# A banded-attention kernel: the turn of the row maxima moved from TensorE to VectorE, and their rows sent by one queue

## The chip, the cores and the metric

One core of a Trainium2 chip. The metric is the device time of one execution in microseconds (us). All times of the kernel before come from one profiled execution or from three timed runs.

## The reference, cut to what matters

```python
# x: [4, 2048, 512] float32; 16 heads of E = 32; windows of W = 128 positions, nw = 16 of them
qkv = layernorm(x) @ w_qkv
q, k, v = split(qkv)                                   # -> [B, H, nw, W, E]
k_ctx = concat([kp[:, :, i:i + nw] for i in range(3)]) # a window, the one before and the one behind
scores = einsum('bhnqe,bhnke->bhnqk', q * scale, k_ctx)
attn = softmax(where(valid, scores, -1e9), axis=-1)    # valid: inside the sequence
x = x + layernorm(einsum('bhnqk,bhnke->bhnqe', attn, v_ctx))
# then a feed-forward part: a gate g per batch from relu(x @ gate_w1.T + b) @ gate_w2.T + b,
# W1, W2 and biases mixed with 8 experts by g, out = gelu(x @ mW1.T + mb1) @ mW2.T + mb2,
x = x + layernorm(ffn(layernorm(x)))
```

The change touches the softmax alone: for each query it needs the largest score of its row before the exponential.

## The kernel before, in words

The program has three stages, one behind the other: the layernorm and the product with w_qkv (up to about 570 us), the attention (573 to 1295 us), and the gate with the mixed feed-forward part. Each of the five engine programs is written out by hand; they meet in semaphores only.

The attention runs over 16 rounds (4 batches by 4 groups of 4 heads) of 8 steps, 128 steps in all, counted by T. A step has two windows of 128 queries and 4 heads, so 8 units. Three pieces of work stand in a step, for different steps of the pipeline:

- **Scores** of the group g = T + 3 (`score`, 8 products): queries by keys, into one of three PSUM banks `ps_score`. VectorE takes the negated maximum of each query from the bank (`reduce`, the line L487), and the product three units on needs that bank again: TensorE waits for `reduced`.
- **Keys** products of the group T (`keys`): the same scores again, but turned, with keys on the partitions and queries along the free axis, so that the exponentials (`weights`, on ScalarE, L415) come out in the layout that the next product wants. The maximum of each query is subtracted by the product itself: below the 96 rows of `q_st` lies row 96 (`STACK`) with the negated maxima, against a row of ones in `k_st`. Queries reach one window past the own one, so the second half of a step's keys products needs the rows of the group T + 1.
- **Values** and **sums** of the group T - 2 (`values`, `sums`, 56 small products of 32 columns), which ScalarE copies out (`copy_out`), TensorE turns (`turn_out`) and VectorE divides by the sums (`normalise`, L499 and L503).

The maxima of the group T + 2 go from the layout "query on the partition" to a row along the free axis in each step in this way: TensorE turns the 128x8 block `neg_max` into `ps_turn[0:8, 0]` behind the values and sums (`turn_max`, L649), VectorE copies it to `max_rows` between its third and its fourth maximum (`copy_rows`, L495), and two DMAs carry it to row 96 of `q_st`, one for each window (`send_row`, L195): the first by ScalarE's queue behind its fifth exponential, the second by the sync engine's queue behind that engine's loads. The first keys products of a group wait for the second row (`rows_landed[1]`), the fifth keys product of the step before (x == 4) waits for the first row alone (`rows_landed[0]`).

The sync engine (SP) issues in a step, in this order: in even steps three loads of `k_st` and in odd steps three of `q_st` (256 KB each) and one of `v_sb` (256 KB), for the next round; the second row; and the store of the normalised output of T - 2, which waits for `norm_done`. The POOL engine adds the exponentials of neighbouring windows for the sums (`first_two`, `third`). In the last 26 steps a part of the gate stage is laid beside the attention (`along`).

Of the kernel before, what the change touches and what calls it, by code (L numbers as in the profile page):

```python
# [43 lines left out]
def attention_programs(nc, ident, eps, power, unused, x, w_qkv, qk_dram, v_dram, o_dram):  # L44
# [18 lines left out]
    with ExitStack() as ctx:  # L63
# [9 lines left out]
        neg_max = sb("neg_max", [P, 2, 2, QH], F32)  # L73
        inv_sum = sb("inv_sum", [P, 2, 2, QH], F32)
        ones = sb("ones", [P, 2, E], F32)
        max_rows = sb("max_rows", [2 * QH, 2, WIN], F32R)
# [72 lines left out]
        max_turned = sem("max_turned")  # L149
        rows_done = sem("rows_done")  # L150
        rows_landed = [[sem(f"rows_landed{i}{p}") for p in range(2)] for i in range(2)]
# [40 lines left out]
        def send_row(eng, g, i):  # L192
            w = 2 * (g % HALF) + i
            eng.wait_ge(rows_done, g + 1)
            eng.dma_start(q_st[STACK:STACK + 1, :, w * WIN:(w + 1) * WIN].bitcast(F32),  # L195
                          max_rows[QH * i:QH * (i + 1), g % 2, :].bitcast(F32)).then_inc(rows_landed[i][g % 2], 16)

        def sync(sp, along):
# [53 lines left out]
            for g in range(QKG):  # L252
                store_qk(PAIRS - 1, 1, g)
                if g == 5:
                    for i in range(2):
                        send_row(sp, 0, i)
            for i in range(2):
                send_row(sp, 1, i)
            store_v(PAIRS - 1, 1)
            for T in range(STEPS + LAG):  # L260
# [17 lines left out]
                if there(T + AHEAD - 1):  # L278
                    send_row(sp, T + AHEAD - 1, 1)
# [10 lines left out]
        def gpsimd(pool, along):  # L290
# [13 lines left out]
            for i in range(2):  # L304
                pool.memset(ones[:, i, i:i + 1], 1.0).then_inc(const_done, 1)
                pool.wait_ge(const_done, 2 + i)
            pool.wait_ge(xn_done, 1)
            pool.memset(k_st[STACK:STACK + 1, :, :].bitcast(F32), 1.0).then_inc(const_done, 1)
# [37 lines left out]
        def scalar(act, along):  # L346
# [78 lines left out]
            for T in range(STEPS + LAG):  # L425
# [5 lines left out]
                for x in range(3, UNITS):  # L431
                    if there(T):
                        weights(T, x)
                    if x == 4 and there(T + AHEAD - 1):
                        send_row(act, T + AHEAD - 1, 0)
                along(T)

        def vector(dve, along):
# [41 lines left out]
            def reduce(g, s):  # L480
# [3 lines left out]
                if s == 0 and g >= 2:  # L484
                    dve.wait_ge(max_turned, g - 1)
# [4 lines left out]
            def copy_rows(g):  # L490
                if g >= 2:
                    for i in range(2):
                        dve.wait_ge(rows_landed[i][g % 2], 16 * (g // 2))
                dve.wait_ge(max_turned, g + 1)
                dve.tensor_copy(max_rows[:, g % 2, :], ps_turn[0:2 * QH, 0, :]).then_inc(rows_done, 1)  # L495
# [38 lines left out]
            chunk(PAIRS - 1, 0)  # L534
            for g in range(GROUPS):
# [4 lines left out]
                if g == 5:  # L540
                    copy_rows(0)
                if g == 9:
                    copy_rows(1)
            for T in range(STEPS + LAG):
                if there(T + AHEAD):
                    for s in range(3):
                        reduce(T + AHEAD, s)
                if there(T + AHEAD - 1):
                    copy_rows(T + AHEAD - 1)
                if there(T + AHEAD):  # L550
                    for s in range(3, UNITS):
# [5 lines left out]
        def tensor(pe, along):  # L557
# [67 lines left out]
            def keys(g, x):  # L625
# [4 lines left out]
                if x == 0 and g % HALF == 0:  # L630
                    pe.wait_ge(rows_landed[0][g % 2], 16 * (g // 2 + 1))
                if x == 0:
                    pe.wait_ge(rows_landed[1][g % 2], 16 * (g // 2 + 1))
                if x == QH and g % HALF != HALF - 1:
                    pe.wait_ge(rows_landed[0][(g + 1) % 2], 16 * ((g + 1) // 2 + 1))
# [3 lines left out]
                else:  # L639
                    pe.wait_ge(v_done, TILES * CHUNKS + x + 1)  # L640
                pe.matmul(ps_keys[x % TRIO][:, 0:(hi - lo) * WIN], k_st[0:STACK + 1, h, w * WIN:(w + 1) * WIN],  # L641
                          q_st[0:STACK + 1, h, lo * WIN:hi * WIN], start=True, stop=True).then_inc(keys_done, 1)

            def turn_max(g):
                pe.wait_ge(reduced, UNITS * (g + 1))
                turned = g - AHEAD - LAG + 1
                if turned > 0:
# [1361 lines left out]
```

## Time and profile before

| | |
|---|---|
| median of 3 runs | 2935.1 us (2927.1 to 2939.1) |
| the profiled execution | 2943.8 us, of which the trace spans 2942.0 us |
| attention, first to last turn of the maxima | 553 to 1266 us, 128 steps |
| one step in the middle (between two copies of the maxima) | 5.2 us |
| TensorE busy | 2870.2 us, 98% of the span |
| VectorE, ScalarE, POOL busy | 1996.6, 1727.7, 854.1 us |

The trace gives each instruction's start and duration, and for each idle time of an engine what ended it. TensorE has two rows there, PE for the products and PEld for the loading of the stationary operand, which runs beside the product before it. SPq and ACTq rows are DMA issues on the queues of the sync engine and of ScalarE: their duration is that of the issue, the landing comes later.

### The profile page before, as it was taken

The numbers are of one execution on the slowest core, as the hardware profiler recorded it, in microseconds if no ns is written. First come the engines' busy times: TensorE is split into PE (matmuls) and PEld (weight loads), VectorE is DVE, ScalarE is ACT, GpSimd is POOL, SyncE is SP. The second block draws the span as 40 slices with busy tenths as digits, with TensorE's granted clock in tenths as the row PEclk, the third lists the DMA queues.
The fourth block names the chain that finished last, engine by engine and source line by source line (L and its number), as shares of the span: only waits on it lengthen the run. The fifth ranks groups of instructions, "written<-read, shape, count | busy, mean of one in ns | idle before, by whom it ended". The sixth has DMA issues, their size and how long they took to land.

```text
span 2942.0 us, 55438 instructions
## 1 busy us (share of the span) xinstructions
PE 2870.2 (98%) x20252; PEld 2380.8 (81%) x20252; DVE 1996.6 (68%) x3769; ACT 1727.7 (59%) x3385; POOL 854.1 (29%) x713
## 2 busy tenths in 40 slices
PE   8999999999999999989989999999999999999998
PEld 6888888888888887767867888788888888888886
DVE  5333333488888887878868766876768766786664
ACT  3222222377776765665636666866667666686666
POOL 1000000188888887974400000500005000040003
PEclk9999999999999999999989999999999999999999
DMA  6555555688888889959998866986769756896632
GB/s 215 184 173 171 185 186 193 218 199 201 198 194 191 201 202 214 225 176 398 390 394 325 284 209 208 356 314 203 248 211 400 270 203 200 288 399 200 232 136 86
DMA packets 361429, 697.10 MB, mean 237 GB/s; under 512 B 26576, under 2 KB 127056, under 8 KB 361184
## 3 DMA queue, kind: packets, MB, share of 16 engines
q1 hardware_dynamic: 335456, 629.63, 67.1%
q10 hardware_dynamic: 17424, 32.24, 3.1%
q0 software_dynamic: 8304, 31.98, 2.7%
q8 instruction: 150, 2.46, 0.4%
q14 instruction: 95, 0.78, 0.1%
HBM read 525.45 MB, written 167.78 MB: 236 GB/s over the span
## 4 chain that ended last, share of the span: by engine, by line
PE 84%; DVE 5%; DMA 5%; ACT 2%; issue 2%; POOL 1%; ACTq 0%; SPq 0%; DVEq 0%; POOLq 0%
PE a_acc L571 17%; PE e_hid L1390 7%; PE e_hid L1392 7%; PE e_hid L1391 7%; PE e_acc L1407 7%; PE e_acc L1409 7%; PE e_acc L1408 7%; PE a_ps_score L622 6%; PE a_ps_keys L641 6%; PE a_ps_out L670 5%; DMA a_gate_att<-o_scratch 2%; DMA a_q_st<-a_max_rows 2%; PE a_ps_out L678 2%; PE a_ps_turn L688 1%; DVE a_gate_stats L1658 1%
## 5 line engine op out<-in xcount | busy, mean ns | idle before, releaser
L1779 DVE SCALAR_TENSOR_TENSOR e_part<-e_ring,e_g_cols,e_part 128x512 f32<-128x512 f32 x896 | 648.5, 779 | 5.7 <-DMA e_ring<-mix_rows 3.3
L487 DVE TENSOR_REDUCE a_neg_max<-a_ps_score 128x1 f32<-128x384 f32 (+1 forms) x1024 | 489.6, 526 | 50.0 <-PE a_ps_score L622 48.7
L323 POOL TENSOR_TENSOR a_total<-a_probs 128x512 f32<-128x512 f32 x256 | 323.7, 1281 | 594.6 <-ACT a_probs L415 594.6
L415 ACT ACTIVATE a_probs<-a_ps_keys 128x384 f32<-128x384 f32 (+1 forms) x1024 | 423.4, 477 | 49.1 <-PE a_ps_keys L641 25.3
L1803 DVE TENSOR_TENSOR e_u_lo<-e_u,e_u_hi 128x512 fp32r<-128x512 f32 x256 | 178.7, 698 | 376.3 <-ACT e_u_hi L1538 376.2
L1534 ACT ACTIVATE e_u<-e_hid,e_mb 128x512 f32<-128x512 f32 x256 | 176.9, 691 | 434.7 <-PE e_hid L1392 422.2
L1263 POOL TENSOR_SCALAR e_var<-e_moments 128x4 f32<-128x4 f32 x15 | 6.7, 446 | 1276.9 <-DVE e_moments L1815 1276.2
L622 PE MATMUL a_ps_score<-a_k_st,a_q_st 96*128 96x384 f32 (+1 forms) x1024 | 335.5, 361 | 4.1 <-DVE a_neg_max L487 3.1
L641 PE MATMUL a_ps_keys<-a_q_st,a_k_st 97*128 97x384 f32 (+1 forms) x1024 | 318.1, 352 | 12.2 <-DMA a_q_st<-a_max_rows 11.1
L333 POOL TENSOR_TENSOR a_total<-a_total,a_probs 128x512 f32<-128x512 f32 x224 | 286.3, 1280 | 55.4 <-ACT a_probs L415 52.8
L467 DVE TENSOR_TENSOR a_qk<-a_acc,a_qk 128x512 fp32r<-128x512 f32 x128 | 88.1, 690 | 308.1 <-ACT a_qk L364 308.1
L1551 ACT ACTIVATE e_sums<-e_acc 128x512 f32<-128x512 f32 x508 | 289.1, 595 | 9.0 <-PE e_acc L1409 5.7
L1562 ACT ACTIVATE e_acc<-e_sums 128x512 f32<-128x512 f32 x448 | 263.7, 613 | 0.0
L364 ACT ACTIVATE a_qk<-a_acc 128x512 fp32r<-128x512 f32 x128 | 76.2, 598 | 258.8 <-PE a_acc L571 255.8
L622 PEld LDWEIGHTS a_ps_score<-a_k_st,a_q_st 96*128 96x128 f32 x1024 | 194.8, 191 | 40.5 <-DVE a_neg_max L487 29.0
L641 PEld LDWEIGHTS a_ps_keys<-a_q_st,a_k_st 97*128 97x128 f32 x1024 | 192.3, 192 | 28.5 <-DMA a_q_st<-a_max_rows 14.0
L571 PE MATMUL a_acc<-a_xt_hi,a_w_hi 128*128 128x512 f32 x508 | 202.5, 399 | 1.6 <-DVE a_w_lo L522 1.0
L1407 PE MATMUL e_acc<-e_wa_hi,e_u_hi 128*128 128x512 f32 x512 | 200.4, 391 | 3.3 <-DVE e_u_lo L1803 3.1
L1390 PE MATMUL e_hid<-e_y_hi,e_wb_hi 128*128 128x512 f32 x512 | 199.8, 390 | 2.5 <-DVE e_wb_lo L1798 2.5
L1407 PE MATMUL e_acc<-e_wb_hi,e_u_hi 128*128 128x512 f32 x512 | 200.1, 391 | 1.3 <-ACT e_acc L1562 1.3
L1390 PE MATMUL e_hid<-e_y_hi,e_wa_hi 128*128 128x512 f32 x512 | 200.5, 392 | 0.0
L1391 PE MATMUL e_hid<-e_y_lo,e_wa_hi 128*128 128x512 f32 x512 | 200.2, 391 | 0.0
(154 smaller groups left out, 6466.7 us busy)
## 6 DMA issues: line engine op xcount, KB each, us to landing
e_ring<-mix_rows SPq DMA_DIRECT2D x558, 512.0 KB, 5.4
qk_scratch<-a_qk SPq DMA_DIRECT2D x128, 512.0 KB, 3.2
a_k_st<-qk_scratch SPq DMA_DIRECT2D x180, 256.0 KB, 4.5
a_q_st<-qk_scratch SPq DMA_DIRECT2D x180, 256.0 KB, 4.4
v_scratch<-a_v SPq DMA_DIRECT2D x64, 256.0 KB, 3.1
a_v_sb<-v_scratch SPq DMA_DIRECT2D x64, 256.0 KB, 5.0
o_scratch<-a_out SPq DMA_DIRECT2D x128, 128.0 KB, 3.1
x_scratch<-a_gate_x POOLq DMA_DIRECT2D x16, 1024.0 KB, 10.1
```

The source lines that it names most:

```text
L323: add = pool.tensor_tensor(total[:, g % 2, i], p[0], p[1], ALU.add)
L333: pool.tensor_tensor(total[:, g % 2, i], total[:, g % 2, i], p[2], ALU.add).then_inc(summed, 1)
L415: act.activation(probs[:, m % PROBS, h, 0:(hi - lo) * WIN], ps_keys[x % TRIO][:, 0:(hi - lo) * WIN], ACT.Exp, scale=SCALE).then_inc(exp_do ...
L487: dve.tensor_reduce(neg_max[:, g % 2, i, h:h + 1], ps_score[y % TRIO][:, 0:(hi - lo) * WIN], AX_X, ALU.max, negate=True).then_inc(reduced, 1)
L571: mm = pe.matmul(out, lhs, rhs, start=(n == 0), stop=(n == len(terms) - 1))
L622: pe.matmul(ps_score[y % TRIO][:, 0:(hi - lo) * WIN], q_st[0:STACK, h, w * WIN:(w + 1) * WIN], k_st[0:STACK, h, lo * WIN:hi * WIN], start= ...
L641: pe.matmul(ps_keys[x % TRIO][:, 0:(hi - lo) * WIN], k_st[0:STACK + 1, h, w * WIN:(w + 1) * WIN], q_st[0:STACK + 1, h, lo * WIN:hi * WIN], ...
L1390: pe.matmul(hid[s % 4][:, :], w_hi(n)[:, 0, cols], y_hi[:, slot, k, :], start=(k == 0), stop=False)
L1391: pe.matmul(hid[s % 4][:, :], w_hi(n)[:, 0, cols], y_lo[:, slot, k, :], start=False, stop=False)
L1407: pe.matmul(acc[t][:, :], u_hi[:, s % 3, cols], w_hi(n)[:, 1, :], start=False, stop=False, skip_group_check=True)
L1551: act.activation(sums[:, runs[r][1], t, :], acc[t][:, :], ACT.Copy).then_inc(copied, 1)
L1779: dve.scalar_tensor_tensor(out=part[:, n % 2, half, :], in0=ring[:, slot, :], scalar=g_cols[:, b, e:e + 1], in1=so_far, op0=ALU.mult, op1= ...
```

## The change

TensorE no longer turns the maxima. VectorE does it in two instructions (`turn_max` in its program). The first multiplies the 128x8 block of maxima into a 128x4x32 tile `spread`: block b keeps the maxima of the partitions 32b to 32b + 31 alone, by a 0/1 mask of four columns that was copied once into the free columns of the PSUM bank `ps_turn`, and the rest is zero. The second turns `spread` (128x128) in blocks of 32x32, which leaves in `max_rows` four rows for each head and window, each zero outside its own 32 queries. Four rows of `q_st` (96 to 99) against four rows of ones in `k_st` then add up to what one row gave before; the keys products contract over 100 rows in place of 97.

VectorE's turn stands at the start of a step, ahead of the first of its eight maxima, and the maxima are no longer cut in two by the copy. Both rows DMAs (now of 16 pieces of 512 bytes in place of 4) are issued by SP behind its loads; ScalarE sends none. There is one semaphore for both: `rows_landed[g % 2]`, counted to 32, which the fifth keys product of the step before waits for. The set-up gains a few small memsets on POOL and one small copy on VectorE.

```diff
@@ -73,5 +73,7 @@
         neg_max = sb("neg_max", [P, 2, 2, QH], F32)
+        spread = sb("spread", [P, P // E, E], F32R)
+        own_block = sb("own_block", [P, P // E], F32)
         inv_sum = sb("inv_sum", [P, 2, 2, QH], F32)
         ones = sb("ones", [P, 2, E], F32)
-        max_rows = sb("max_rows", [2 * QH, 2, WIN], F32R)
+        max_rows = sb("max_rows", [P, 2, WIN], F32R)
         q_st = sb("q_st", [P, QH, SEQ], F32R)
@@ -148,5 +150,6 @@
         reduced = sem("reduced")
-        max_turned = sem("max_turned")
+        spread_done = sem("spread_done")
+        mask_done = sem("mask_done")
         rows_done = sem("rows_done")
-        rows_landed = [[sem(f"rows_landed{i}{p}") for p in range(2)] for i in range(2)]
+        rows_landed = [sem(f"rows_landed{p}") for p in range(2)]
         keys_done = sem("keys_done")
@@ -191,7 +194,8 @@
 
-        def send_row(eng, g, i):
-            w = 2 * (g % HALF) + i
+        def send_rows(eng, g):
             eng.wait_ge(rows_done, g + 1)
-            eng.dma_start(q_st[STACK:STACK + 1, :, w * WIN:(w + 1) * WIN].bitcast(F32),
-                          max_rows[QH * i:QH * (i + 1), g % 2, :].bitcast(F32)).then_inc(rows_landed[i][g % 2], 16)
+            for i in range(2):
+                w = 2 * (g % HALF) + i
+                eng.dma_start(q_st[STACK:STACK + P // E, :, w * WIN:(w + 1) * WIN].bitcast(F32),
+                              max_rows[i:P:E // QH, g % 2, :].bitcast(F32)).then_inc(rows_landed[g % 2], 16)
 
@@ -254,6 +258,4 @@
                 if g == 5:
-                    for i in range(2):
-                        send_row(sp, 0, i)
-            for i in range(2):
-                send_row(sp, 1, i)
+                    send_rows(sp, 0)
+            send_rows(sp, 1)
             store_v(PAIRS - 1, 1)
@@ -278,3 +280,3 @@
                 if there(T + AHEAD - 1):
-                    send_row(sp, T + AHEAD - 1, 1)
+                    send_rows(sp, T + AHEAD - 1)
                 if T == 0:
@@ -306,4 +308,12 @@
                 pool.wait_ge(const_done, 2 + i)
+            pool.wait_ge(const_done, 3)
+            pool.memset(spread[:, :, :].bitcast(F32), 0.0).then_inc(const_done, 1)
+            pool.wait_ge(const_done, 4)
+            pool.memset(own_block[:, :], 0.0).then_inc(const_done, 1)
+            for b in range(P // E):
+                pool.wait_ge(const_done, 5 + b)
+                pool.memset(own_block[b * E:(b + 1) * E, b:b + 1], 1.0).then_inc(const_done, 1)
+            pool.wait_ge(const_done, 9)
             pool.wait_ge(xn_done, 1)
-            pool.memset(k_st[STACK:STACK + 1, :, :].bitcast(F32), 1.0).then_inc(const_done, 1)
+            pool.memset(k_st[STACK:STACK + P // E, :, :].bitcast(F32), 1.0).then_inc(const_done, 1)
 
@@ -433,4 +443,2 @@
                         weights(T, x)
-                    if x == 4 and there(T + AHEAD - 1):
-                        send_row(act, T + AHEAD - 1, 0)
                 along(T)
@@ -484,3 +492,3 @@
                 if s == 0 and g >= 2:
-                    dve.wait_ge(max_turned, g - 1)
+                    dve.wait_ge(spread_done, g - 1)
                 dve.wait_ge(scored, y + 1)
@@ -489,8 +497,14 @@
 
-            def copy_rows(g):
+            def turn_max(g):
+                dve.wait_ge(reduced, UNITS * (g + 1))
+                if g >= 1:
+                    dve.wait_ge(rows_done, g)
+                dve.tensor_tensor(spread[:, :, :].rearrange("p b (h i) -> p b i h", h=QH)[:, :, 0:2],
+                                  neg_max[:, g % 2].unsqueeze(1).to_broadcast([P, P // E, 2, QH]),
+                                  ps_turn[:, 0, 0:P // E].unsqueeze(2).unsqueeze(3).to_broadcast([P, P // E, 2, QH]),
+                                  ALU.mult).then_inc(spread_done, 1)
+                dve.wait_ge(spread_done, g + 1)
                 if g >= 2:
-                    for i in range(2):
-                        dve.wait_ge(rows_landed[i][g % 2], 16 * (g // 2))
-                dve.wait_ge(max_turned, g + 1)
-                dve.tensor_copy(max_rows[:, g % 2, :], ps_turn[0:2 * QH, 0, :]).then_inc(rows_done, 1)
+                    dve.wait_ge(rows_landed[g % 2], 32 * (g // 2))
+                dve.transpose(max_rows[:, g % 2, :].bitcast(F32), spread[:, :, :].bitcast(F32).rearrange("p b c -> p (b c)")).then_inc(rows_done, 1)
 
@@ -534,2 +548,5 @@
             chunk(PAIRS - 1, 0)
+            dve.wait_ge(const_done, 10)
+            dve.tensor_copy(ps_turn[:, 0, 0:P // E], own_block[:, :]).then_inc(mask_done, 1)
+            dve.wait_ge(mask_done, 1)
             for g in range(GROUPS):
@@ -540,13 +557,10 @@
                 if g == 5:
-                    copy_rows(0)
+                    turn_max(0)
                 if g == 9:
-                    copy_rows(1)
+                    turn_max(1)
             for T in range(STEPS + LAG):
-                if there(T + AHEAD):
-                    for s in range(3):
-                        reduce(T + AHEAD, s)
                 if there(T + AHEAD - 1):
-                    copy_rows(T + AHEAD - 1)
+                    turn_max(T + AHEAD - 1)
                 if there(T + AHEAD):
-                    for s in range(3, UNITS):
+                    for s in range(UNITS):
                         reduce(T + AHEAD, s)
@@ -630,7 +644,5 @@
                 if x == 0 and g % HALF == 0:
-                    pe.wait_ge(rows_landed[0][g % 2], 16 * (g // 2 + 1))
-                if x == 0:
-                    pe.wait_ge(rows_landed[1][g % 2], 16 * (g // 2 + 1))
+                    pe.wait_ge(rows_landed[g % 2], 32 * (g // 2 + 1))
                 if x == QH and g % HALF != HALF - 1:
-                    pe.wait_ge(rows_landed[0][(g + 1) % 2], 16 * ((g + 1) // 2 + 1))
+                    pe.wait_ge(rows_landed[(g + 1) % 2], 32 * ((g + 1) // 2 + 1))
                 x += 8 * g
@@ -640,12 +652,4 @@
                     pe.wait_ge(v_done, TILES * CHUNKS + x + 1)
-                pe.matmul(ps_keys[x % TRIO][:, 0:(hi - lo) * WIN], k_st[0:STACK + 1, h, w * WIN:(w + 1) * WIN],
-                          q_st[0:STACK + 1, h, lo * WIN:hi * WIN], start=True, stop=True).then_inc(keys_done, 1)
-
-            def turn_max(g):
-                pe.wait_ge(reduced, UNITS * (g + 1))
-                turned = g - AHEAD - LAG + 1
-                if turned > 0:
-                    pe.wait_ge(norm_done, turned)
-                pe.transpose(ps_turn[0:2 * QH, 0, :], neg_max[:, g % 2].rearrange("p w h -> p (w h)"), ident[:, :])\
-                  .then_inc(max_turned, 1)
+                pe.matmul(ps_keys[x % TRIO][:, 0:(hi - lo) * WIN], k_st[0:STACK + P // E, h, w * WIN:(w + 1) * WIN],
+                          q_st[0:STACK + P // E, h, lo * WIN:hi * WIN], start=True, stop=True).then_inc(keys_done, 1)
 
@@ -683,3 +687,3 @@
                 pe.wait_ge(out_copied, g + 1)
-                pe.wait_ge(rows_done, min(g + LAG + AHEAD, STEPS))
+                pe.wait_ge(spread_done, min(g + LAG + AHEAD, STEPS))
                 if g >= 1:
@@ -723,3 +727,3 @@
             chunk(PAIRS - 1, 0)
-            pe.wait_ge(const_done, 4)
+            pe.wait_ge(const_done, 10)
             for g in range(GROUPS):
@@ -728,6 +732,2 @@
                     score(y // UNITS, y % UNITS)
-                if g == 5:
-                    turn_max(0)
-                if g == 9:
-                    turn_max(1)
             for T in range(STEPS + LAG):
@@ -742,4 +742,2 @@
                 along(T)
-                if there(T + AHEAD - 1):
-                    turn_max(T + AHEAD - 1)
                 scores(T, [3])
```

In VectorE's program, in the middle of the attention, the instructions stand before in this order (`a_neg_max` rows are the maxima, L499 and L503 the division of the output):

```order
L487 TENSOR_REDUCE a_neg_max<-a_ps_score 128x1 x3
L495 CAST a_max_rows<-a_ps_turn 8x128
L487 TENSOR_REDUCE a_neg_max<-a_ps_score 128x1 x5
L499 RECIPROCAL a_inv_sum<-a_ps_turn 128x8
L503 TENSOR_TENSOR a_out<-a_ps_turn,a_inv_sum 128x256
```

and now in this:

```order
L502 TENSOR_TENSOR a_spread<-a_neg_max,a_ps_turn 128x4x2x4
L509 STREAM_TRANSPOSE a_max_rows<-a_spread 128x128
L495 TENSOR_REDUCE a_neg_max<-a_ps_score 128x1 x8
L513 RECIPROCAL a_inv_sum<-a_ps_turn 128x8
L517 TENSOR_TENSOR a_out<-a_ps_turn,a_inv_sum 128x256
```

One copy has gone from the middle of the maxima, two instructions have come in front of them.

On the queue of the sync engine, an odd step and an even step in the middle of the attention stand before in this order:

```order
L183 DMA a_q_st<-qk_scratch 32x4x512 x3
L230 DMA a_v_sb<-v_scratch 128x4x128
L195 DMA a_q_st<-a_max_rows 1x4x128
L236 DMA o_scratch<-a_out 128x2x128
L183 DMA a_k_st<-qk_scratch 32x4x512 x3
```

and now in this:

```order
L186 DMA a_q_st<-qk_scratch 32x4x512 x3
L234 DMA a_v_sb<-v_scratch 128x4x128
L199 DMA a_q_st<-a_max_rows 4x4x128 x2
L240 DMA o_scratch<-a_out 128x2x128
L186 DMA a_k_st<-qk_scratch 32x4x512 x3
```

The row that ScalarE sent has joined the other one behind the loads, and each is four rows wide.

On ScalarE's queue one window of exponentials stands before as

```order
L415 ACTIVATE a_probs<-a_ps_keys 128x384 x2
L195 DMA a_q_st<-a_max_rows 1x4x128
L415 ACTIVATE a_probs<-a_ps_keys 128x384 x6
L422 ACTIVATE a_out_t<-a_ps_out 128x384
```

and the DMA in it is gone.

## Rows read from the trace of the kernel before

**Rows 1.** Page, part 1: engine, busy time, share of the span, instructions

```profile
PE 2870.2 (98%) x20252; PEld 2380.8 (81%) x20252; DVE 1996.6 (68%) x3769; ACT 1727.7 (59%) x3385; POOL 854.1 (29%) x713
```

**Rows 2.** Windows view, attention: PE, PEld, DVE, ACT, POOL busy; clock; DMA share

```profile
573.00:1276.00 703.00, 686.99 (x10326) 581.01 (x10326) 577.70 (x1411) 486.82 (x1152) 605.46 (x487) 0.99 0.84 200
```

**Rows 3.** Timeline of VectorE: start, us, line, tiles, count, idle before

```profile
1004.91 0.28 DVE L495 CAST a_max_rows<-a_ps_turn 8x128 fp32r<-8x128 f32 x1 [0.75 <-PE a_ps_turn L649]
...
1007.76 0.42 DVE L503 TENSOR_TENSOR a_out<-a_ps_turn,a_inv_sum 128x256 f32<-128x256 f32 x1
1008.10 1.48 DVE L487 TENSOR_REDUCE a_neg_max<-a_ps_score 128x1 f32<-128x384 f32 x3
1010.11 0.28 DVE L495 CAST a_max_rows<-a_ps_turn 8x128 fp32r<-8x128 f32 x1 [0.53 <-PE a_ps_turn L649]
1010.31 2.50 DVE L487 TENSOR_REDUCE a_neg_max<-a_ps_score 128x1 f32<-128x384 f32 x5
1012.74 0.20 DVE L499 RECIPROCAL a_inv_sum<-a_ps_turn 128x8 f32<-128x8 f32 x1
1012.97 0.42 DVE L503 TENSOR_TENSOR a_out<-a_ps_turn,a_inv_sum 128x256 f32<-128x256 f32 x1
```

**Rows 4.** Timeline of TensorE, same step: loads (PEld) and products (PE)

```profile
1009.70 0.08 PEld L649 LDWEIGHTS a_ps_turn<-ident,a_neg_max 128*8 128x8 f32 x1 [0.20 <-DVE a_neg_max L487]
1009.70 0.19 PEld L622 LDWEIGHTS a_ps_score<-a_k_st,a_q_st 96*128 96x128 f32 x1
1009.73 0.42 PE L622 MATMUL a_ps_score<-a_k_st,a_q_st 96*128 96x384 f32 x1
...
1010.90 0.19 PEld L622 LDWEIGHTS a_ps_score<-a_k_st,a_q_st 96*128 96x128 f32 x1 [0.19 <-DVE a_neg_max L487]
```

**Rows 5.** Waits view, whole span: who for whom, us, times, longest

```profile
DVE a_max_rows L495 <- PE a_ps_turn L649: 96.5, 120, 3.3
...
PEld a_ps_score L622 <- DVE a_neg_max L487: 29.0, 119, 1.9
...
PEld a_ps_keys L641 <- DMA a_q_st<-a_max_rows: 14.0, 9, 3.0
```

**Rows 6.** Timeline of SP's queue: issue start, duration

```profile
1008.21 0.38 SPq L236 DMA_DIRECT2D o_scratch<-a_out  x1
1008.64 2.67 SPq L183 DMA_DIRECT2D a_q_st<-qk_scratch  x3
1011.35 0.69 SPq L230 DMA_DIRECT2D a_v_sb<-v_scratch  x1
1012.08 0.58 SPq L195 DMA_DIRECT2D a_q_st<-a_max_rows  x1
1013.42 0.39 SPq L236 DMA_DIRECT2D o_scratch<-a_out  x1
1013.85 1.62 SPq L183 DMA_DIRECT2D a_k_st<-qk_scratch  x3
```

**Rows 7.** DMA view, windows 1000.5:1000.9 and 1011.2:1011.6: issues, us to landing

```profile
a_v_sb<-v_scratch SPq DMA_DIRECT2D x1, 256.0 KB, 4.8
...
a_v_sb<-v_scratch SPq DMA_DIRECT2D x1, 256.0 KB, 4.9
```

**Rows 8.** Timelines: v load issued on SP, keys products of the next step on PE

```profile
1000.62 0.43 SPq L230 DMA_DIRECT2D a_v_sb<-v_scratch  x1
...
1005.09 0.51 PE L641 MATMUL a_ps_keys<-a_q_st,a_k_st 97*128 97x384 f32 x2
...
1015.56 0.51 PE L641 MATMUL a_ps_keys<-a_q_st,a_k_st 97*128 97x384 f32 x2
```

**Rows 9.** Timeline of ScalarE and its queue

```profile
1010.73 0.58 ACTq L195 DMA_DIRECT2D a_q_st<-a_max_rows  x1
```

**Rows 10.** Lines by form, VectorE: L1679 and L1658 in 573:1276, then L1679 behind 1300

```profile
L1679 DVE SCALAR_TENSOR_TENSOR a_gate_shift<-a_gate_moments,a_gate_rstd 128x4 f32<-128x4 f32 x2 | 5.5, 2760 | 0.0
L1658 DVE BATCH_NORM_STATS2 a_gate_stats<-a_gate_att 128x6 f32<-128x512 f32 x12 | 8.2, 682 | 0.0
...
L1679 DVE SCALAR_TENSOR_TENSOR a_gate_shift<-a_gate_moments,a_gate_rstd 128x4 f32<-128x4 f32 x13 | 2.5, 196 | 0.4
```

More of the change, by code:

```diff
@@ L540, in vector @@
                 if g == 5:
-                    copy_rows(0)
+                    turn_max(0)
                 if g == 9:
-                    copy_rows(1)
+                    turn_max(1)
             for T in range(STEPS + LAG):
+                if there(T + AHEAD - 1):
+                    turn_max(T + AHEAD - 1)
                 if there(T + AHEAD):
-                    for s in range(3):
-                        reduce(T + AHEAD, s)
-                if there(T + AHEAD - 1):
-                    copy_rows(T + AHEAD - 1)
-                if there(T + AHEAD):
-                    for s in range(3, UNITS):
+                    for s in range(UNITS):
                         reduce(T + AHEAD, s)
@@ L742, in tensor @@
                 along(T)
-                if there(T + AHEAD - 1):
-                    turn_max(T + AHEAD - 1)
                 scores(T, [3])
```

## The prediction, on record before the changed kernel ran

> **What bounds the kernel now.** I read the page's first part, then the attention alone by its windows, then three steps of it as a timeline, engine by engine, and last the waits and the DMA landings. TensorE is busy 98% of the span [rows 1], and in the attention 687.0 of 703 us, at a granted clock of 0.99, its upper level of 2.4 GHz. VectorE has 577.7 us there, ScalarE 486.8, POOL 605.5, and the DMA engines are busy to 84% [rows 2]. So TensorE sets the end. Outside the attention the change has only small set-up work that lies beside 500 us of other stages; I cost it at nothing.
>
> The reader is to see two things in the step that begins with the copy at 1004.91 and ends with the next at 1010.11, 5.20 us on [rows 3]. First, VectorE waits: 0.53 us before the copy L495, for TensorE's turn of the maxima, which stands behind all values and sums; 96.5 us in all, 120 times [rows 3, 5]. Second, TensorE pays for it a little later. The fourth score product has run from 1009.73 to 1010.15 [rows 4], but its maximum starts at 1010.31, behind the copy [rows 3]. The seventh score product needs that bank: its load of operands waits 0.19 us, until 1010.90 [rows 4]. Such waits are 29.0 us in 119 cases, nearly one for each of the 128 steps [rows 5]. They are what the change can give back to TensorE.
>
> **TensorE's turn.** 128 products of 128x128 against an 8-column operand go. The trace says that they hid well: the loads of the turn and of the score product behind it both start at 1009.70, and the score product starts 0.03 us later [rows 4]. Without the turn that score product must first load its own operand, 0.19 us long, which now lies partly under the turn. So I take 0.0 us for the turn, with 0 and 0.1 us as bounds; a little of this may show, but not 0.28 us a step.
>
> **The copy.** Without it the fourth maximum can start when its score product has ended, 1010.15 plus about 0.04 us of signalling (my estimate: 1012.97 - 1012.74 - 0.20 = 0.03 between the two dependent instructions of rows 3), so at 1010.18 in place of 1010.31 [rows 3, 4]. The seventh score product moves by the same 0.13 us, and of its wait of 0.19 us some 0.06 stays. Bounds: 0 and 0.19 us a step. I take 0.13: over about 124 steps (128 without the first and last few) **-16 us**.
>
> **VectorE's new work** must fit. A step now holds, from start to start: five maxima 2.43 us (1010.31 to 1012.74), reciprocal 0.23, division 0.34 (1007.76 to 1008.10), three maxima about 1.40: 4.40 us [rows 3]. New are the mask product, 32 elements a partition from PSUM, and the turn, 128 elements from SBUF. For the first the nearest rows are the reciprocal, 0.20 us, and the division, 0.42 us for 256 elements [rows 3]: 0.20 plus 0.03 for the wait between the two. For the second: the copy of 128 elements, 0.28 us, of which 0.20 show up to the next start (1010.11 to 1010.31) [rows 3], and 0.68 us for the statistics over 512 elements [rows 10]. I take 0.25 us, as it is nearest to the copy. Together 0.5 us, at worst 0.9. That gives 4.9 us of a 5.07 us step, still in front of the bound; at 0.9 us VectorE would need 5.3 and the gain is gone in narrow steps (+0.1 us each). The maxima that wait behind it are the first three of the step, which TensorE needs only after its values and sums. Cost 0 at the value taken.
>
> **ScalarE** loses a DMA issue of 0.58 us [rows 9]. Its exponentials are not what TensorE waits for in these rows; I take nothing for it.
>
> **The rows on SP's queue.** Here the change costs. Before, the fifth keys product of a step waited only for the first row, issued by ScalarE at 1010.73 [rows 9]. The row that SP issues at 1012.08, behind three q loads and one v load [rows 6], was needed half a step later still. Now both stand behind the loads, and both are needed at the fifth keys product. In an odd step: the v load is issued at 1011.35 and lands 4.9 us later, at 1016.25; the keys pair with the fifth product started at 1015.56 [rows 6 to 8]. In the pair of steps before it: 1000.62 + 4.8 = 1005.42 against 1005.09 [rows 7, 8]. If the rows land no earlier than the load ahead of them they are 0.7 and 0.3 us late, 0.5 on average, and the second DMA may add up to its own issue, 0.58 us [rows 6]. If they overtake it they are in time. A row DMA is 8 KB against 256 KB, so I do not charge the whole landing, and take half: 0.25 us late against the old time, bounds 0 and 1.1 us. Even steps carry no v load and their rows can leave when the k loads are issued, which is earlier than before; I take nothing. The odd wait cannot be made up: the q loads start behind a store that waits for the end of VectorE's step two steps before (1008.21) [rows 6], so rows, fifth keys product, end of step and next odd step are one ring. Of it only the part behind the fifth keys product gets 0.13 us shorter. Per pair of steps the ring gives 0.25 - 0.13 = +0.12 us where TensorE alone would give -0.26. Over 62 pairs: **+7 us** in place of -16. VectorE's earlier turn does not help an odd row, since that waits for SP, not for `rows_done`.
>
> **The sum.** 2943.8 us of the profiled execution + 7 = 2951; that execution lies 8.7 us above the median of the three runs, 2935.1, so for the median I forecast **2942 us**. Less than 0.5% (about 15 us) cannot be told from no change here.
>
> **Rivals.**
>
> *The rows come in time.* Then only the gain stands: -16 us, 2919 us. For it: in the kernel before the rows delayed loads of keys products 9 times only (14.0 us) [rows 5]. Against: that wait was for a row that had left 0.6 us before the v load [rows 6, 9]. Chance 0.22.
>
> *The rows wait in full.* 0.5 us late, -0.13, over 62 pairs: +23 us, 2958 us; with the second DMA's 0.58 us whole: +59 us, 2994 us. This is the case that ends slower. It decides from 0.13 us of lateness on. For it speaks the DMA share of 84% [rows 2], which leaves few gaps to overtake in. Chance 0.2.
>
> *VectorE's turn waits for POOL.* In the attention POOL adds nearly without a pause (605 of 703 us) [rows 2]. An instruction of VectorE with two inputs in SBUF took 2.76 us there and 0.20 us where POOL is idle, while the statistics, with one input, took 0.68 [rows 10]. The mask product reads one of its inputs from PSUM, as the division does, whose 0.42 us are steady. The turn has one input, but source and target are both SBUF. Should it be held like L1679, by 0.6 us or more, VectorE needs 5.5 us a step: some +0.35 us over 124 steps, +43 us, 2978 us, and twice that if POOL loses as much. Since the statistics are not held, chance 0.1.
>
> The Trainium skill ("SBUF — State Buffer", SBUF: two separate sides) says that VectorE and GpSimd share a port pair as an exclusive lock for VectorE instructions in a two-port mode or with two SBUF inputs. By that rule, the trace agrees: L1679 is held, L1658 is not. The skill's "Vector Engine (DVE) Microarchitecture Reference" (5.1) lists copy, cast and tensor_scalar as enabled for that mode and not the turn, which speaks against this rival; its "VectorE: DVE Perf Modes" (The three transpose paths) gives 311 ns for a 128x128 bf16 turn, with which the sum would be the same.
>
> *The forecast*, some lateness that about eats the gain: chance 0.48.
>
> **How the numbers follow.** Faster by over 0.5% (under 2920 us) needs nearly the whole gain: most of the first rival, 0.17. Slower (over 2950): the second and third rival nearly whole and an end of the forecast's, 0.34. The rest, 0.49, is within 0.5%. The range goes from a little below the first rival, 2916, to between the second one's two prices, 2972; what lies outside is about 0.08 below and 0.12 above.
>
> **What would show it.** In the new profile: no L649; a turn and a mask product on VectorE of about 0.25 and 0.2 us; fewer than 29 us of waits of score products for maxima; VectorE's idle time in the middle of a step down from 96.5 us; and, as the test of the forecast, waits of keys products for the rows at each second step, of some 0.2 to 0.5 us, 20 us or so in all. Steps of 5.07 us with no such wait would mean that the first rival holds. A turn of 0.8 us or more would mean the third. I would be wrong altogether if TensorE's turn did cost more than it seems, or if ScalarE's freed 0.58 us brought the exponentials, and with them the keys products, forward.

## The result and the profile after

The changed kernel takes 2946.3 us (median of 8 runs, 2944.8 to 2952.4) against 2933.8 us of the kernel before in 8 runs beside it: a ratio of 1.0042, 95% interval 1.0032 to 1.0051, some 12 us slower. The forecast for the same comparison was +7 us. The profiled execution spans 2950.6 us, 8.6 more than before; below, "the trace" is that one. It is the slowest of its eight runs, 6 us above their median, and the trace of before is of a run 10 us above its median, so the medians, and not two spans, say what the change costs.

The page's first part, the answer to [rows 1]:

```profile
PE 2859.3 (97%) x20124; PEld 2382.3 (81%) x20124; DVE 2024.2 (69%) x3898; ACT 1727.7 (59%) x3385; POOL 855.9 (29%) x719
```

TensorE has 128 instructions and 11 us of busy time less, VectorE 129 instructions and 28 us more. VectorE's new pair, from the lines view of the attention (573 to 1290 us):

```profile
L509 DVE STREAM_TRANSPOSE a_max_rows<-a_spread 128x128 f32<-128x128 f32 x126 | 39.2, 311 | 4.4
L502 DVE TENSOR_TENSOR a_spread<-a_neg_max,a_ps_turn 128x32 fp32r<-128x32 f32 x126 | 25.7, 204 | 0.1
```

0.31 and 0.20 us, with a spread of no more than 0.04 us over all 128. VectorE's timeline in a step with 40 values products (most steps have 48 and are some 0.2 us longer), to be read against [rows 3], whose step also has 40:

```profile
1016.07 0.20 DVE L502 TENSOR_TENSOR a_spread<-a_neg_max,a_ps_turn 128x32 fp32r<-128x32 f32 x1
1016.30 0.31 DVE L509 STREAM_TRANSPOSE a_max_rows<-a_spread 128x128 f32<-128x128 f32 x1
1016.54 1.45 DVE L495 TENSOR_REDUCE a_neg_max<-a_ps_score 128x1 f32<-128x384 f32 x3
1018.15 2.52 DVE L495 TENSOR_REDUCE a_neg_max<-a_ps_score 128x1 f32<-128x384 f32 x5 [0.16 <-PE a_ps_score L636]
1020.58 0.20 DVE L513 RECIPROCAL a_inv_sum<-a_ps_turn 128x8 f32<-128x8 f32 x1
1020.82 0.42 DVE L517 TENSOR_TENSOR a_out<-a_ps_turn,a_inv_sum 128x256 f32<-128x256 f32 x1
1021.16 0.20 DVE L502 TENSOR_TENSOR a_spread<-a_neg_max,a_ps_turn 128x32 fp32r<-128x32 f32 x1
```

From pair to pair 5.09 us, where the step of [rows 3] took 5.20; the fourth maximum waits only for its own score product, and a step without a late row is about 0.1 us shorter. The waits of the attention, in the order of [rows 5] (who for whom, us, times, longest):

```profile
DVE a_neg_max L495 <- PE a_ps_score L636: 93.9, 167, 3.3
...
PEld a_ps_keys L653 <- DMA a_q_st<-a_max_rows: 47.0, 40, 3.6
...
PEld a_ps_score L636 <- DVE a_neg_max L495: 13.6, 63, 0.8
...
PEld a_ps_keys L653 <- ACT a_probs L425: 3.9, 14, 0.6
```

The waits for maxima have halved, 29.0 to 13.6 us. The waits for the rows have gone from 14.0 to 47.0 us. Of these, counted step by step in the timelines, 43.6 us in 38 of the 40 cases are for rows that SP sent in an odd step, and 19.5 us in 10 cases lie behind 1110 us, mostly where the gate's part runs beside the attention. In full at one place: SP's queue, then TensorE's loads of operands in the step that needs those rows.

```profile
1070.34 2.52 SPq L186 DMA_DIRECT2D a_q_st<-qk_scratch  x3
1072.91 0.43 SPq L234 DMA_DIRECT2D a_v_sb<-v_scratch  x1
1073.38 1.14 SPq L199 DMA_DIRECT2D a_q_st<-a_max_rows  x2
1075.22 0.39 SPq L240 DMA_DIRECT2D o_scratch<-a_out  x1
```

```profile
1077.21 0.19 PEld L636 LDWEIGHTS a_ps_score<-a_k_st,a_q_st 96*128 96x128 f32 x1
1078.63 0.30 PEld L653 LDWEIGHTS a_ps_keys<-a_q_st,a_k_st 100*128 100x128 f32 x2 [1.23 <-DMA a_q_st<-a_max_rows]
```

The rows had been ready in SBUF since 1070.35 (the turn started at 1070.04 and took 0.31). The DMA view of that moment gives the v load in front of them 5.2 us to landing:

```profile
a_v_sb<-v_scratch SPq DMA_DIRECT2D x1, 256.0 KB, 5.2
```

1072.91 + 5.2 = 1078.11, and the keys product goes on at 1078.63: the profile has no landing of the rows themselves, but the wait for them ends only after the load has landed, not before it. The chain of work that ended last, cut to 573 to 1276 us, before and after (its shares by line):

```profile
by line: PE a_ps_score L622 25.0%; PE a_ps_keys L641 23.5%; PE a_ps_out L670 22.9%; DMA a_q_st<-a_max_rows 7.4%; PE a_ps_out L678 7.2%; PE a_ps_turn L688 5.4%; PE a_ps_turn L649 3.2%; DVE a_neg_max L487 1.6%; issue 1.1%; ACT a_probs L415 0.
```

```profile
by line: DMA a_q_st<-a_max_rows 21.0%; PE a_ps_score L636 15.4%; PE a_ps_keys L653 15.3%; PE a_ps_out L674 12.8%; SPq L186 8.3%; issue 4.8%; DVE a_neg_max L495 4.3%; PE a_ps_out L682 4.0%; PE a_ps_turn L692 3.2%; SPq L199 2.4%; SPq L234 2.0
```

Before, TensorE's own work made up most of the chain, and the rows' DMA 7.4% of it. Now it runs for a fifth of the time through the rows' DMA, and with 8.3% through SP's issue of loads (L186), as it should if rows, keys product and loads form the ring over two steps that the prediction describes.

### The profile page after: what moved, and what is told of

Read it like the earlier page. It is cut to its first block, busy times and chain, and to the rows that moved or that the text cites. A ratio compares the mean times of both kernels' runs of the same rounds, so it can differ in the third digit from the quotient of the medians.

```text
span 2950.6 us, 55211 instructions
## 1 busy us (share of the span) xinstructions
PE 2859.3 (97%) x20124; PEld 2382.3 (81%) x20124; DVE 2024.2 (69%) x3898; ACT 1727.7 (59%) x3385; POOL 855.9 (29%) x719
## 4 chain that ended last, share of the span: by engine, by line
PE 76%; DMA 8%; DVE 6%; SPq 3%; issue 3%; ACT 2%; POOL 2%; ACTq 0%; DVEq 0%; POOLq 0%
PE a_acc L585 17%; PE e_acc L1405 7%; PE e_hid L1388 7%; PE e_hid L1389 7%; PE e_hid L1390 7%; PE e_acc L1407 7%; PE e_acc L1406 7%; DMA a_q_st<-a_max_rows 5%; PE a_ps_score L636 4%; PE a_ps_keys L653 4%; PE a_ps_out L674 3%; DMA a_gate_att<-o_scratch 3%; SPq L186 2%; DVE a_neg_max L495 1%; POOL a_gate_x L1229 1%
## 5 line engine op out<-in xcount | busy, mean ns | idle before, releaser
L653 PE MATMUL a_ps_keys<-a_q_st,a_k_st 100*128 100x384 f32 (+1 forms) x1024 | 317.6, 352 | 36.4 <-DMA a_q_st<-a_max_rows 35.1
L636 PE MATMUL a_ps_score<-a_k_st,a_q_st 96*128 96x384 f32 (+1 forms) x1024 | 325.0, 358 | 1.4 <-DVE a_neg_max L495 1.3
L653 PEld LDWEIGHTS a_ps_keys<-a_q_st,a_k_st 100*128 100x128 f32 x1024 | 190.2, 191 | 54.4 <-DMA a_q_st<-a_max_rows 47.0
L1406 PE MATMUL e_acc<-e_wa_lo,e_u_hi 128*128 128x512 f32 x512 | 200.1, 391 | 0.0
```

Of the source, the lines that this page charges most:

```text
L636: pe.matmul(ps_score[y % TRIO][:, 0:(hi - lo) * WIN], q_st[0:STACK, h, w * WIN:(w + 1) * WIN], k_st[0:STACK, h, lo * WIN:hi * WIN], start= ...
L1406: pe.matmul(acc[t][:, :], u_hi[:, s % 3, cols], w_lo(n)[:, 1, :], start=False, stop=False, skip_group_check=True)
```

## The experiments

All ratios are to the kernel before, run beside each kernel on the same chip. The waits are those of one traced execution each. Theory A: the rows on SP's queue behind its loads eat a real gain. Theory B: VectorE's turn or the four-row pieces cost the time.

**Who sends the first row** (e1). ScalarE sends it again, behind its fifth exponential:

```diff
+                    if x == 4 and there(T + AHEAD - 1):
+                        send_rows(act, T + AHEAD - 1, (0,))
-                    send_rows(sp, T + AHEAD - 1)
+                    send_rows(sp, T + AHEAD - 1, (1,))
```

with the separate semaphores and waits of before.

> The changed kernel, with the first row of each step sent by ScalarE's queue behind its fifth exponential as before, the second by the sync engine behind its loads, and the old separate waits. Theory A (the rows that must pass SP's loads eat the gain): the waits of the keys products for the rows fall from 47 us back to about 14, the steps without a wait keep their length (5.3 us in place of 5.42), so about 25 us less than the changed kernel: a ratio to the kernel before of about 0.995. Theory B (VectorE's turn itself, or the four-row pieces, cost the time): the ratio stays at 1.003 to 1.005. ScalarE has its issue of 0.58 us back; if that issue was what held the keys products, the ratio is 1.00.

Measured: 2931.5 us, ratio 0.9992 (0.9983 to 1.0001). Some 15 us back, but not the 0.995 that A expected; it is the third outcome of the expectation, 1.00. Nor is all of it the queue's doing, since this kernel has the separate waits too: with them alone the ratio is already 1.0006 (e4 below), so that the other queue is worth 0.14%, little more than the noise of the two ratios. Its waits:

```profile
PEld a_ps_keys L658 <- DMA a_q_st<-a_max_rows: 24.9, 24, 2.7
...
PEld a_ps_keys L658 <- ACT a_probs L425: 11.9, 59, 0.6
```

The waits for rows do not fall to 14 us, and the keys products now wait 11.9 us for exponentials, 59 times, where the changed kernel has 3.9. ScalarE's issue (0.55 us in that trace) is not hidden here. It wasn't wholly hidden before either: that kernel has 7.0 us of the same waits, and with ScalarE's issue taken out (e3 below) 2.8. The waits for maxima are 13.3 us here, as low as in the changed kernel, with ScalarE's issue back: that gain does not come from the missing issue.

**Rows ahead of the loads** (e2).

```diff
             for T in range(STEPS + LAG):
+                if there(T + AHEAD - 1):
+                    send_rows(sp, T + AHEAD - 1)
...
-                if there(T + AHEAD - 1):
-                    send_rows(sp, T + AHEAD - 1)
                 if T == 0:
```

> The changed kernel, with both rows issued by the sync engine ahead of its loads of the same step in place of behind them. Theory A: hardly any wait of the keys products for rows outside the last 26 steps, so the whole gain shows: 12 to 18 us less than the kernel before, a ratio of 0.994 to 0.996, and below the run with ScalarE's row if its issue costs anything. Theory B: 1.003 to 1.005. A third outcome: the loads, now 1.6 us later, become what the score products wait for; then waits for q and k loads appear and the ratio is 1.00 or more.

Measured: 2923.6 us, ratio 0.9965 (0.9952 to 0.9979), the span of its trace 2913.2 us. The traced run is the fastest of the five, 9 us below their median, so its waits are the kernel's at its best.

```profile
PEld a_ps_score L636 <- DVE a_neg_max L495: 14.1, 64, 0.9
...
PEld a_ps_score L636 <- DMA a_q_st<-qk_scratch: 7.0, 5, 2.5
...
PEld a_ps_keys L653 <- DMA a_q_st<-a_max_rows: 4.3, 4, 1.4
```

The same DMAs, the same queue, the same VectorE: only the order on the queue differs, and 43 us of waits for rows and 0.8% of the time (23 us) are gone. A had expected 0.994 to 0.996; the waits for q loads in the middle line are part of the third outcome. Theory B falls here: the turn costs 0.31 us in this trace too, and pieces of four rows are in it as well.

**One part of the change alone** (e3): the kernel before, TensorE's turn kept, both rows by SP behind its loads, two semaphores.

```diff
-                    send_row(sp, T + AHEAD - 1, 1)
+                    for i in range(2):
+                        send_row(sp, T + AHEAD - 1, i)
-                    if x == 4 and there(T + AHEAD - 1):
-                        send_row(act, T + AHEAD - 1, 0)
```

> The kernel before, with one part of the change alone: both rows are sent by the sync engine behind its loads, each with its own semaphore, and ScalarE sends none. TensorE still turns the maxima. Theory A: this alone costs; the fifth keys product now waits for a row behind the v load at part of the odd steps. Each is one row and not four, and the steps are 0.1 us longer, so less than the 33 us more of waits in the changed kernel: 10 to 25 us more than before, a ratio of 1.003 to 1.009. Theory B: within 0.2% of the kernel before.

Measured: 2938.7 us, 1.0015 (1.0006 to 1.0024): slower, clear of noise, but by less than the 1.003 that A asked for at least, and inside the 0.2% of B. Taken alone this run does not decide between them. Its waits for rows are 20.7 us in 25 cases, 14.0 in 9 before; the waits for maxima (24.3) stay near the 29.0 of before.

**Two waits in place of one** (e4), on the changed kernel.

```diff
-                    pe.wait_ge(rows_landed[g % 2], 32 * (g // 2 + 1))
+                    pe.wait_ge(rows_landed[0][g % 2], 16 * (g // 2 + 1))
+                if x == 0:
+                    pe.wait_ge(rows_landed[1][g % 2], 16 * (g // 2 + 1))
                 if x == QH and g % HALF != HALF - 1:
-                    pe.wait_ge(rows_landed[(g + 1) % 2], 32 * ((g + 1) // 2 + 1))
+                    pe.wait_ge(rows_landed[0][(g + 1) % 2], 16 * ((g + 1) // 2 + 1))
```

> The changed kernel with one semaphore for each of the two row DMAs again: the fifth keys product waits for the first DMA alone, the second one is waited for at the first keys product of its step. Both are still sent by the sync engine behind its loads. If the second DMA is what comes late (it is issued 0.57 us behind the first), a good part of the 33 us of added waits goes: a ratio near 0.998. If both land together, behind the loads, hardly anything changes: 1.002 to 1.004. I expect the second.

Measured: 2937.4 us, 1.0006 (0.9996 to 1.0017), with 31.9 us of waits for rows. I had expected 1.002 to 1.004, and it is 0.36% better than the changed kernel: the wait for the second DMA, which the fifth keys product doesn't need, makes up about 10 of the 12 us lost.

**The joint wait without the wide rows** (e7): e3 with the fifth keys product waiting for both DMAs.

```diff
-                    pe.wait_ge(rows_landed[0][(g + 1) % 2], 16 * ((g + 1) // 2 + 1))
+                    for i in range(2):
+                        pe.wait_ge(rows_landed[i][(g + 1) % 2], 16 * ((g + 1) // 2 + 1))
```

> The kernel before, with both rows sent by the sync engine behind its loads, and the fifth keys product waiting for both, as in the changed kernel; the turn is TensorE's, each DMA carries one row. Against the run in which that product waited for the first DMA alone (1.0015): if waiting for the second DMA is worth about 10 us here too, as it was with the four-row pieces, 1.004 to 1.006. If the four-row pieces are what makes the second DMA late, 1.0015 to 1.003.

Measured: 2943.9 us, 1.0030 (1.0019 to 1.0041). The joint wait costs 0.15% here and 0.36% with pieces of four rows; each is a difference of two ratios with intervals of 0.1%. That it costs is shown for the wide rows; for single rows it is at the edge of the noise, and that wide rows make it worse is not shown.

**TensorE's turn put back, its result unused** (e5), on e2.

```diff
+            def idle_turn(g):
+                pe.wait_ge(spread_done, g + 1)
...
+                pe.transpose(ps_turn[0:2 * QH, 1, :], neg_max[:, g % 2].rearrange("p w h -> p (w h)"), ident[:, :])
...
                 along(T)
+                if there(T + AHEAD - 1):
+                    idle_turn(T + AHEAD - 1)
```

> The kernel with both rows ahead of the loads (ratio 0.9965), and TensorE's turn of the maxima put back where it stood, its result unused: 126 products more, nothing waits for them. The prediction costed that turn at nothing, with 0.1 us as bound. By it: within 2 us of the kernel with the rows ahead, 0.9965 to 0.997. If the turn did cost TensorE what a 128-column product takes in a dense run (0.11 us, from the spacing of the three output turns), 12 to 14 us more: 1.001.

Measured: 2924.1 us, 0.9955 (0.9938 to 0.9972). 126 turns cost nothing that can be told: from the low end of e2's interval to the high end of this one it is 6 us, an estimate of 0.05 us a turn at most. Taking them from TensorE gained nothing by itself. The waits for maxima stay low (6.0 us) with the turn back.

**Rows ahead, with TensorE's late turn** (e8): e3 with both sends at the head of SP's step.

```diff
             for T in range(STEPS + LAG):
+                if there(T + AHEAD - 1):
+                    for i in range(2):
+                        send_row(sp, T + AHEAD - 1, i)
                 if T == 2:
```

> The kernel before, with both rows sent by the sync engine ahead of its loads, nothing else changed. TensorE's turn comes 1.4 to 1.8 us later in a step than VectorE's, so the loads behind the rows start some 1.9 us plus 1.2 us of issues later than in the kernel before. Theory A (the early turn on VectorE is what makes rows ahead of the loads worth it): waits for q, k or v loads appear or the steps keep their 5.4 us, ratio 0.999 to 1.006. Theory C (the order on the queue is all, whoever turns): 0.9965 as with VectorE's turn.

Measured: 2963.2 us, 1.0093 (1.0078 to 1.0108), worse than every other kernel and than A's 1.006. SP's queue, and the waits:

```profile
1000.81 0.44 SPq L236 DMA_DIRECT2D o_scratch<-a_out  x1
1002.90 1.21 SPq L195 DMA_DIRECT2D a_q_st<-a_max_rows  x2
1004.15 1.39 SPq L183 DMA_DIRECT2D a_q_st<-qk_scratch  x3
```

```profile
PEld a_ps_score L621 <- DMA a_q_st<-qk_scratch: 37.5, 41, 4.7
```

SP stands idle from 1001.25 to 1002.90 for the late rows, the loads behind them start that much later, and the score products wait 37.5 us for loads of q, while the waits for rows are down to 0.3 us. In e2 the same gap is 0.1 us:

```profile
1003.45 0.38 SPq L240 DMA_DIRECT2D o_scratch<-a_out  x1
1003.92 1.16 SPq L199 DMA_DIRECT2D a_q_st<-a_max_rows  x2
1005.13 1.72 SPq L186 DMA_DIRECT2D a_q_st<-qk_scratch  x3
```

So theory C (order alone) falls: it takes the early turn and the early place on the queue together. That the early turn has to be VectorE's is not shown; TensorE's turn was not tried at an earlier place.

**Rows between the q and the v loads** (e10).

```diff
+                if there(T + AHEAD - 1):
+                    send_rows(sp, T + AHEAD - 1)
                 n, c = divmod((T - 5) // 2, 4)
                 if T >= 5 and T % 2 == 1 and n + 1 < ROUNDS:
                     sp.wait_ge(pv_done, T - 2)
                     load_v(n + 1, c)
-                if there(T + AHEAD - 1):
-                    send_rows(sp, T + AHEAD - 1)
```

> The changed kernel, with both rows behind the three k or q loads as before but ahead of the v load of the odd steps. The prediction priced a late row by the landing of the v load in front of it. If that is the load that matters, most of the 47 us of waits for rows goes: a ratio of 0.997 to 0.999. If a row is late behind any load, since the DMA engines are still busy with the q loads, about half of them stay: 1.000 to 1.003.

Measured: 2931.7 us, 0.9991 (0.9980 to 1.0003), between the two outcomes, with 21.0 us of waits for rows in 22 cases. Passing the one v load gives back 0.5% of 0.8%, so it is the load that matters most. The rest is not the q loads' alone: about half of these waits, 10.3 us in 9 cases, are for rows sent in even steps, behind the k loads.

**VectorE's turn between the maxima** (e6), where the copy stood.

```diff
-                if there(T + AHEAD - 1):
-                    turn_max(T + AHEAD - 1)
                 if there(T + AHEAD):
-                    for s in range(UNITS):
+                    for s in range(3):
+                        reduce(T + AHEAD, s)
+                if there(T + AHEAD - 1):
+                    turn_max(T + AHEAD - 1)
+                if there(T + AHEAD):
+                    for s in range(3, UNITS):
                         reduce(T + AHEAD, s)
```

> The changed kernel, with VectorE's mask product and turn between the third and the fourth maximum, where the copy stood, in place of ahead of the first. VectorE idles 0.38 us there in the changed kernel and the two take 0.47 us. If the gain in steps without a late row (5.42 to 5.31 us) comes from the fourth maximum no longer standing behind a copy, half of it or more goes, since the turn now stands there: 3 to 8 us more than the changed kernel, 1.005 to 1.007. The rows of odd steps wait for the loads anyway. If the gain comes from ScalarE's missing issue or from TensorE's missing turn, the ratio stays at 1.004.

Measured: 2944.9 us, 1.0026 (1.0014 to 1.0038). I expected it slower than the changed kernel, and it is not; the waits for maxima are 13.7 us, as low as there. Its timeline says why:

```profile
1001.84 1.48 DVE L495 TENSOR_REDUCE a_neg_max<-a_ps_score 128x1 f32<-128x384 f32 x3
1003.23 0.20 DVE L502 TENSOR_TENSOR a_spread<-a_neg_max,a_ps_turn 128x32 fp32r<-128x32 f32 x1
1003.47 0.31 DVE L509 STREAM_TRANSPOSE a_max_rows<-a_spread 128x128 f32<-128x128 f32 x1
1004.13 2.54 DVE L495 TENSOR_REDUCE a_neg_max<-a_ps_score 128x1 f32<-128x384 f32 x5 [0.36 <-PE a_ps_score L639]
```

The turn starts as the third maximum ends and is over before the fourth one's score product is. What delayed the fourth maximum before was not that something stood there, but that the copy waited for TensorE's turn, which came behind the values and sums. Of the other sources of the gain, e5 rules out TensorE's turn as such, and e1 ScalarE's issue.

**Rows ahead in odd steps alone** (e12).

```diff
             for T in range(STEPS + LAG):
+                if T % 2 == 1 and there(T + AHEAD - 1):
+                    send_rows(sp, T + AHEAD - 1)
...
-                if there(T + AHEAD - 1):
+                if T % 2 == 0 and there(T + AHEAD - 1):
                     send_rows(sp, T + AHEAD - 1)
```

> The changed kernel, with the rows ahead of the loads in odd steps alone (those with q loads and the v load) and behind the k loads in even steps. With both ahead (0.9965) score products waited 7.0 us for q loads in 5 cases. If only the odd steps had late rows, this is as fast as with both ahead or up to 5 us faster: 0.995 to 0.997. If even steps had late rows too, waits for rows come back: 0.998 to 1.000.

Measured: 2926.9 us, 0.9965 (0.9953 to 0.9978), the same as e2. But the waits for rows are back:

```profile
PEld a_ps_keys L655 <- DMA a_q_st<-a_max_rows: 21.0, 19, 4.5
```

Of these 21.0 us, 20.5 in 18 cases are for rows sent in even steps, behind the k loads. One of them: its rows leave SP at 1035.25 and the keys product goes on 5.8 us later.

```profile
1033.76 1.44 SPq L186 DMA_DIRECT2D a_k_st<-qk_scratch  x3
1035.25 1.14 SPq L199 DMA_DIRECT2D a_q_st<-a_max_rows  x2
```

```profile
1041.06 0.30 PEld L655 LDWEIGHTS a_ps_keys<-a_q_st,a_k_st 100*128 100x128 f32 x2 [0.47 <-DMA a_q_st<-a_max_rows]
```

So rows of even steps are late as well once the odd steps no longer hold everything up; by the ratios this costs nothing that can be told. With the same 21.0 us of waits e10 stands at 0.9991: the sum of the waits for rows does not give the time, and why it costs so little here is open. What the ratios show is that the place of the odd steps' rows is worth the 0.8%.

## Why the prediction was right, point by point

- **The gain**, -16 us (0.13 us a step). In the steps shown 0.11 us (5.20 to 5.09), about -14 us over 124 steps; by the runs -10 us (e2, 0.9965), where some waits for rows and q loads are still in. Right in kind and nearly in size; the mechanism was as told, the waits for maxima fell from 29.0 to 13.6 us. e6 makes it sharper: it is the copy's wait for TensorE that went. VectorE's own waits did not go but moved: 96.5 us for the turn and 19.0 for score products before, 93.9 for score products now.
- **TensorE's turn at nothing.** Right, shown by e5. The 0.28 us that its row carries are no time on the path.
- **VectorE's new work**, 0.5 us in the step. Measured 0.20 + 0.31 us with starts that overlap the neighbours: 0.47 us from the mask product to the next maximum (1016.07 to 1016.54). It fits, as costed.
- **POOL's hold on the turn**, a rival at 0.1: did not happen. The turn takes 0.311 to 0.314 us beside a busy POOL. By the rule of the Trainium skill ("Vector Engine (DVE) Microarchitecture Reference", 5.1), which does not list the turn for the two-port mode, the trace agrees.
- **ScalarE's issue at nothing.** Not quite: keys products waited 7.0 us for exponentials before, 2.8 with the issue taken out (e3), 3.9 in the changed kernel and 11.9 with it put back (e1). Some 3 us of waits went by it that the forecast left out; what they are worth in time no run shows alone.
- **The rows on SP's queue**, "take half: 0.25 us late". It stood for 23 us (from -16 to +7). By the runs it cost that: from e2 to the changed kernel is 0.77%, 23 us, give or take 5. The trace's waits for rows grew by more, 33.0 us. But the working behind the 23 us is not what the runs show, and that the total fits is partly luck. I had 0.25 us at every second step; the trace has waits for rows of 38 of some 62 odd steps, 1.15 us on average and up to 3.6. At the place shown the rows did not overtake the load at all, where I had taken half, and e4 shows that the second DMA, which I left inside the bounds, is worth about 10 us. The ring over two steps fits what is seen, SP's issue of loads stands in the chain with 8.3%, but no run breaks it alone. Even steps have only 3.5 us of these waits in the changed kernel. They are not safe from them: e12 has 20.5 us there, at no cost in time that can be told.
- **The sum**: +7 forecast, +12 measured. Of the trace's waits, +33.0 for rows, -15.4 for maxima and -3.1 for exponentials (7.0 before in the same view, 3.9 after) add up to about +14 us, against 8.6 us between the two spans and 12 us between the medians. That the forecast is 5 us off is within what single terms leave open (-16 against -10 to -14, 23 against 18 to 28); which of them was off is not resolved.

The rival "the rows come in time" was the one to build: e2 has it, with -10 us against the -16 forecast for it.

## What to carry to other kernels

The small transfer that the next step waits for landed here behind the 256 KB load that its queue had issued before it, so place such a transfer by the landing of what is ahead of it, not by its own size, and let a consumer wait only for the DMA that it reads (0.36% here). Moving TensorE's turn off the busiest engine gained nothing, as it was hidden there; what gained is the wait that VectorE had for it. The early result and the early place on the queue paid only together: 1.0042 with the early turn and rows behind the loads (1.0006 with separate waits), 1.0093 with rows ahead and the late turn, and 0.9965 with both. And sums of waits in one trace are a guide to the place, not to the price: two kernels with 21.0 us of waits for rows differ by 0.26%.

## What the runs showed of the hardware that I had not expected

- At the place shown, two DMAs of 8 KB issued behind a 256 KB load on the same queue ended their reader's wait 0.5 us after that load had landed (1078.63 against 1078.11), 5.2 us after the first of them was issued (1073.38); ahead of the loads they hardly kept anyone waiting (4.3 us in 4 cases, in e2's trace).
- VectorE turns 128x128 float32 in blocks of 32x32 in 0.311 us, without a visible hold by a POOL that is busy for 595 of the attention's 703 us.
- A 128-column turn on TensorE with an 8-column operand between dense products shows 0.27 us in its row and cost nothing that can be told (0.9955 with it, within 0.17% either way; 0.9965 without, within 0.14%).
